# Attention and a routed expert layer on one core: the first five shared steps inside attention's last five, a third group routed in attention

## The chip, the cores and the metric

One core of a Trainium2 chip runs the whole kernel as one program. The metric is the device time of a run in microseconds (us). Five engines work side by side, each through a queue of its own in order: PE (products and transposes), ACT (activations and copies), DVE (vector operations), POOL (some vector work, and the indirect DMAs) and SP (plain DMAs). They meet only at semaphores.

## What is computed

```python
def reference(x, ctx, Wq, Wk, Wv, Wo, bo, gate_w, gate_b, w1, b1, w3, b3, w2, b2, sw1, ...):
    # x (4, 1024, 256), ctx (4, 64, 192), 16 heads of 64, 8 experts, top 2, H = 352, all fp32
    x = x + xattn(layernorm(x), ctx)          # cross attention, softmax over 64 keys
    xf = layernorm(x).reshape(4096, 256)
    scores = softmax(xf @ gate_w.T)           # (4096, 8)
    idx = top_k(scores + gate_b, 2)
    rw = zeros((4096, 8)).at[arange, idx].add(scores[idx])
    h = silu((xf @ w1[e] + b1[e]) * (xf @ w3[e] + b3[e]))
    y = sum_e rw[:, e] * (h @ w2[e] + b2[e])
    z = silu((xf @ sw1 + sb1) * (xf @ sw3 + sb3)) @ sw2 + sb2     # shared expert, all tokens
    return x + y + z
```

## The kernel before

The 4096 tokens are 32 tiles of 128 (NT = 32). Every product is done as three products of rounded parts: each operand is split into a high part (`...h`, an ACT copy to fp32r) and a low part (`...l`, DVE: the value less the high part).

After a short prelude, which folds the weights into `AU`, comes **attention**, a software pipeline written out in steps s = 0 to 37 (`tile_step`, lag 6). Every engine goes through the same steps. In step s PE does the scores of tile s-1, the gate product of tile s-6 (L1309, out of `xn2T`), the transposes of the probabilities of tile s-3, the output product of tile s-4 and, last, the transposes of the normalised tile s-5 (L1360, `xn2`). ACT copies `xn2T` (L740), makes `xn2` (L747), `pTh` (L768) and the exponentials. DVE does maxima and sums, `pTl`, the residual and the statistics, and copies the logits (L1007). POOL computes the reciprocal roots (L601 to L605) and normalises the probabilities (`prob`, L612, once a step). SP loads `xin`, `xres`, and stores. From step 33 on no scores are left: the last five steps, 33 to 37, are the drain.

**Routing** of a group of tiles is six stages on DVE (`route`), one a step, each a chain in which every operation waits for the one before (`link`). Its stage 1 needs an exponential of ACT, stage 5 the running counts of PE (`ranks`). At its end the slots are cast, and POOL scatters two records a tile into the table `slots_scratch` (L658, at most three in flight). Groups 0 to 7 and 8 to 15 run in steps 14 to 19 and 22 to 27. The other 16 tiles, the rest, are routed after attention. Scatters go at one tile a step from step 20, and stop in step 30 with tile 10.

Idle places in attention also take the expert weights: SP loads `w13_raw` (steps 13 to 17, 21 to 23) and `w2_raw` (24 to 32), ACT makes `w13h` of experts 0 to 4 in steps 33 to 37 (L871), DVE `w13l` of experts 0 to 2 in 35 to 37 (L1120).

**The FFN** is 103 steps of one tile (`unit_step`): 20 shared tiles, 71 routed units of 128 gathered rows, 12 shared tiles. In step s PE does the second product of tile s-4 (nine matmuls), the transposes of tile s (L1407, into bank 0), the transposes of the hidden rows of s-3 (L1415), the first product of tile s-1 (twelve matmuls). ACT copies `yrow` of s-4, `uxTh` of s, `hTh` of s-3, and does Silu of s-2; DVE `uxTl`, `hTl`, `uv` (L1161) and `hid` (L1164). In steps 1 to 17 ACT and DVE also split the other weights (`high2`, `low2`, `high13`, `low13`).

PE starts the FFN when all of attention is done, and puts the rest's `ranks` behind its step 2; DVE puts the rest's stages between its steps 0 to 3. After the last scatter SP reads each unit's slots (L534), POOL gathers the rows (L707), and PE's step 20, the first of a routed unit, waits for the first gather. The scatters that are left over after attention stand in this loop of POOL, those of tiles 11 to 15 first:

```python
            for t in range(scattered_by(NT), REST[0]):
                for k in range(TOP):
                    scatter_record(t, k)
            pool.wait_ge(slot_ok, len(GROUPS) + 1)
```

## Time and profile before

| | |
|---|---|
| median of 3 runs | 738.7 us (736.76 to 742.82) |
| the profiled execution | 745.34 us, its span 743.6 us |
| granted TensorE clock, mean | 0.977 |
| PE busy | 676.8 us (91%) |
| DVE busy | 527.4 us (71%) |
| POOL busy | 431.5 us (58%) |
| ACT busy | 402.4 us (54%) |
| attention's last gate product | 335.19 us from the span's start |
| first routed step on PE | 427.18 us |

The busy share counts what an engine executes, waits left out; PE's is modelled and says that it had a matmul in its pipe, not that it ran at its peak. The chain of waits goes back from the last instruction to what released each one. Times in the rows are from the span's start.

### The profile page before, as it was taken

What the parts mean: (1) busy time and instruction counts of PE and PEld (TensorE: products, weight loads), DVE (VectorE), ACT (ScalarE), POOL (GpSimd) and SP (SyncE); (2) the same over time, 40 slices, a digit from 0 to 9 for tenths busy, and PEclk for the clock granted to TensorE, in tenths of its full rate; (3) what the DMA queues carried; (4) which work ended last, traced back from release to release, by engine and by line L of the source; (5) the groups of instructions that cost most, each with busy time, mean ns of one, the idle gap of its engine ahead of it and who ended that gap; (6) DMA issues with size and microseconds to landing.
All of it is one profiled execution on the core that took longest, in us unless ns stands there. A gap on an engine that the chain in (4) does not pass through costs nothing.

```text
span 743.6 us, 16844 instructions
## 1 busy us (share of the span) xinstructions
PE 676.8 (91%) x4645; PEld 632.3 (85%) x4646; DVE 527.4 (71%) x1080; ACT 402.4 (54%) x1307; POOL 431.5 (58%) x514
## 2 busy tenths in 40 slices
PE   4996799999898989966799599999999999999996
PEld 3785699998897879865799599999999999999995
DVE  4875788888976868747789456666666666666686
ACT  3985778777766657655543234444444444444342
POOL 5352674545567768434546417776676777676273
PEclk9999999999999999987999889999999999999999
DMA  8202222235427756426241125554444444455496
GB/s 243 81 1 71 65 76 83 83 109 176 120 58 140 128 111 108 124 76 188 46 70 37 36 61 73 75 76 73 74 76 71 71 71 73 75 96 104 91 386 253
DMA packets 71940, 74.83 MB, mean 101 GB/s; under 512 B 21178, under 2 KB 65572, under 8 KB 71876
## 3 DMA queue, kind: packets, MB, share of 16 engines
q1 hardware_dynamic: 52372, 50.51, 26.0%
q0 software_dynamic: 15760, 18.96, 15.9%
q10 hardware_dynamic: 3744, 4.59, 1.8%
q8 instruction: 30, 0.49, 0.3%
q14 instruction: 34, 0.28, 0.1%
HBM read 47.22 MB, written 26.81 MB: 100 GB/s over the span
## 4 chain that ended last, share of the span: by engine, by line
PE 75%; DMA 11%; issue 4%; DVE 4%; POOL 3%; ACT 2%; SPq 0%; ACTq 0%; POOLq 0%; DVEq 0%
PE ps L1235 62%; DMA slots_scratch<-record,slot 8%; PE ps L1415 4%; PE ps L1332 3%; PE ps L1407 3%; POOL slots_scratch L658 2%; DMA xin<-in_x 1%; PE ps L1309 1%; DMA wq_sb<-in_L_xattn_Wq 1%; PE ps L1322 1%; ACT prob L776 1%; DVE hmax L1021 1%; PE ps L1360 1%; DVE st L1056 0%; DVE x L1054 0%
## 5 line engine op out<-in xcount | busy, mean ns | idle before, releaser
L714 POOL DMA_INDIRECT acc_scratch<-yrow,slots x71 | 112.1, 1579 | 71.0 <-ACT yrow L902 70.7
L902 ACT ACTIVATE yrow<-ps,slots 128x256 f32<-128x256 f32 x71 | 33.8, 476 | 147.8 <-PE ps L1235 133.2
L1235 PE MATMUL ps<-AU,xTh 128*128 128x512 f32 x256 | 96.8, 423 | 9.2 <-DVE xTl L1034 9.2
L1235 PE MATMUL ps<-AU,pTh 128*128 128x256 f32 x512 | 101.3, 290 | 0.0
L1235 PE MATMUL ps<-w13h,uxTh 128*128 x284 | 97.7, 344 | 0.0
L1161 DVE TENSOR_TENSOR uv<-ps,b 128x704 f32<-128x704 f32 x71 | 63.3, 892 | 47.6 <-PE ps L1235 45.8
L658 POOL DMA_INDIRECT slots_scratch<-record,slot x64 | 67.5, 1054 | 45.0 <-DMA slots_scratch<-record,slot 32.6
L1235 PE MATMUL ps<-w13h,uxTl 128*128 x284 | 91.6, 322 | 0.0
L1235 PE MATMUL ps<-w13l,uxTh 128*128 x284 | 91.3, 321 | 0.0
L707 POOL DMA_INDIRECT xrow<-xn_scratch,slots x71 | 69.9, 985 | 26.3 <-issue 20.7
L1235 PEld LDWEIGHTS ps<-AU,pTh 128*128 128x128 f32 x512 | 82.4, 191 | 0.0
L776 ACT ACTIVATE prob<-ps,nmax 128x64 f32<-128x64 f32 x256 | 76.7, 338 | 6.8 <-DVE nmax L1024 6.8
L1143 DVE TENSOR_TENSOR uxTl<-ps,uxTh 128x256 fp32r<-128x256 f32 x103 | 43.6, 423 | 51.1 <-ACT uxTh L916 42.4
L1235 PE MATMUL ps<-AU,pTl 128*128 128x256 f32 x256 | 72.8, 284 | 0.0
L612 POOL TENSOR_TENSOR prob<-prob,hinv 128x1024 f32<-128x1024 f32 x32 | 61.0, 1905 | 19.4 <-DVE hinv L1003 19.3
L1235 PEld LDWEIGHTS ps<-AU,xTh 128*128 128x128 f32 x256 | 49.6, 194 | 19.1 <-DVE xTl L1034 10.2
L1235 PE MATMUL ps<-w2h,hTh 128*128 x213 | 63.0, 296 | 0.0
L1164 DVE TENSOR_TENSOR hid<-uv 128x352 f32<-128x352 f32 x103 | 59.9, 581 | 3.5
L1235 PE MATMUL ps<-w2l,hTh 128*128 x213 | 60.3, 283 | 0.0
L1235 PE MATMUL ps<-w2h,hTl 128*128 x213 | 60.0, 282 | 0.0
L776 ACT ACTIVATION_READ_ACCUMULATOR prob<-ps,nmax 128x1 f32 x256 | 59.2, 231 | 0.0
L1148 DVE TENSOR_TENSOR hTl<-ps,hTh 128x384 fp32r<-128x384 f32 x103 | 57.2, 556 | 1.8 <-ACT hTh L921 1.4
(237 smaller groups left out, 1989.3 us busy)
## 6 DMA issues: line engine op xcount, KB each, us to landing
sums<-acc_scratch SPq DMA_DIRECT2D x16, 512.0 KB, 10.5
w_raw<-in_L_ffn_w SPq DMA_DIRECT2D x16, 352.0 KB, 4.1
xin<-in_x SPq DMA_DIRECT2D x32, 128.0 KB
xres<-in_x SPq DMA_DIRECT2D x32, 128.0 KB
acc_scratch<-x SPq DMA_DIRECT2D x32, 128.0 KB
xn_scratch<-xn SPq DMA_DIRECT2D x32, 128.0 KB
xrow<-xn_scratch SPq DMA_DIRECT2D x32, 128.0 KB, 3.1
out_x<-sums SPq DMA_DIRECT2D x7, 512.0 KB, 12.0
```

Source lines behind the costliest of these rows:

```text
L612: pool.tensor_tensor(heads, heads, hinv[:, p, :].unsqueeze(2).to_broadcast([P, HEADS, NK]), ALU.mult).then_inc(norm_ok, 1)
L658: pool.indirect_dma_start(slots_dram, bass.IndirectOffsetOnAxis(ap=slot[:, k, t:t + 1], axis=0), record[:, t, k, :], None).then_inc(scat_o ...
L707: pool.indirect_dma_start(xrow[:, m, :], None, xn2_dram, bass.IndirectOffsetOnAxis(ap=slots[:, u, 0:1], axis=0)).then_inc(gather_in[m], 16)
L714: pool.indirect_dma_start(acc_dram[u % 2], bass.IndirectOffsetOnAxis(ap=slots[:, u, 0:1], axis=0), yrow[:, m % YRING, :], None, compute_op ...
L776: act.activation(prob[:, p, h * NK:(h + 1) * NK], ps[:, s_bank(p) + h // 8, h % 8 * NK:(h % 8 + 1) * NK], ACT.Exp, bias=nmax[:, p, h - HS: ...
L902: act.activation(yrow[:, y, :], ps[:, 6 + m % 2, 0:D], ACT.Copy, scale=slots[:, bass.ds(u, 1), 1].bitcast(F32)).then_inc(y_ok, 1)
L1143: dve.tensor_tensor(uxTl[:, p, :], ps[:, 0, 0:D], f32(uxTh[:, p, :]), ALU.subtract).then_inc(uxTl_ok, 1)
L1148: dve.tensor_tensor(hTl[:, :], ps[:, 5, 0:H3], f32(hTh[:, :]), ALU.subtract).then_inc(hTl_ok, 1)
L1161: dve.tensor_tensor(uv[:, :, :], ps[:, 1 + 2 * p:3 + 2 * p, 0:H], bias, ALU.add).then_inc(bias_ok, 1)
L1164: dve.tensor_tensor(hid[:, p, 0:H], uv[:, 0, :], uv[:, 1, :], ALU.mult).then_inc(z_ok, 1)
L1235: last = pe.matmul(out, stationary(k, a), moving(k, b), start=(k == 0 and i == 0), stop=(k == n - 1 and i == len(PARTS) - 1 and not more))
L1415: last = pe.transpose(ps[:, 5, k * P:(k + 1) * P], hid[:, p, k * P:(k + 1) * P], ident[:, :])
```

## The change

- **Shared steps in the drain.** `DRAIN` = 33. In attention's steps 33 to 37 every engine does, after its part of attention, the FFN's step s-33. PE's transposes of the first five shared tiles go to bank 7 instead of bank 0 (`x_bank`). PE then does steps 5 to 7 before the rest's `ranks`; DVE puts the rest's stages between its steps 5 to 8. `hid`'s padding is set by POOL in step 33.
- **A third group.** Tiles 16 to 19 are routed in steps 28 to 33 (`BEGIN`); the rest is 12 tiles.
- **Scatters** go on through step 36: tiles 0 to 16 in attention, 17 to 19 right after it, 20 to 31 when the rest's slots are there.
- **Loads and splits.** w1 and w3 of experts 5 to 7 are loaded one half a step in steps 20 to 25 (before: whole in 21 to 23), w2 in 26 to 33. `high2` moves from FFN steps 1 to 4 to 5 to 8, `low13` of experts 3 and 4 to steps 6 and 7, `low2` to 8 to 15. Shared rows 8 to 11 are loaded ahead of the biases.
- **Layout.** `xres`, `x2`, `xn2`, `xn2T` move below `xin`, `b13` and `gv` move up.

```diff
-    GROUPS = ((0, 8), (8, 16))
-    REST = (16, NT)
-    NREST = NT - 16
+    GROUPS = ((0, 8), (8, 16), (16, 20))
+    BEGIN = (14, 22, 28)
+    REST = (20, NT)
+    NREST = NT - 20
...
+        DRAIN = NT + 1
+        XBANK7 = NT + 6 - DRAIN
...
+        def x_bank(t):
+
+            return 7 if isinstance(t, int) and t < XBANK7 else 0
...
-                if s in (21, 22, 23):
-                    load_w13(s - 16)
...
+                if 20 <= s < 20 + 2 * (E - EARLY13):
+                    load_w13((s - 20) // 2 + EARLY13, s % 2)
...
-                for s in range(min(step, NT - 2) + 1):
-                    routed = max([b for _, b in GROUPS if b + 6 + STAGES <= s], default=0)
+                for s in range(step + 1):
+                    routed = max([b for (_, b), first in zip(GROUPS, BEGIN) if first + STAGES <= s], default=0)
...
-            for t in range(scattered_by(NT), REST[0]):
+            for t in range(scattered_by(NT + 4), REST[0]):
+                pool.wait_ge(slot_ok, len(GROUPS))
...
                 tile_step(s, par)
+                if s >= DRAIN:
+                    unit_step(s - DRAIN, s - DRAIN)
                 if 33 <= s < 33 + EARLY13:
                     high13(s - 33)
...
             act.wait_ge(lg_ok, NT)
-            act.wait_ge(hid_one, 2)
-            act.wait_ge(zero_out, 16 * (NB // QUAD + 3))
-            unit_steps(act, unit_step)
+            for half in xn2_out + x2_out:
+                act.wait_ge(half, before(NT))
+            act.wait_ge(rt_sub, len(GROUPS) + 1)
+            act.activation(rest_score[:, :, :], rest_marked[:, 0, :, :], ACT.Exp).then_inc(rt_exp, 1)
+            unit_steps(act, unit_step, begun=NT + 6 - DRAIN)
...
+            def begin_step(s, par):
+                tile_step(s, par)
+                if s == DRAIN:
+                    pe.wait_ge(exp_ok, NT)
+                    pe.wait_ge(sw_lo, 2)
+                if s >= DRAIN:
+                    unit_step(s - DRAIN, s - DRAIN)
+
+            steps(NT, 0, 6, begin_step)
             pe.wait_ge(lg_ok, NT)
-            pe.wait_ge(sw_lo, 2)
-            for s in range(3):
+            for s in range(NT + 6 - DRAIN, 8):
                 unit_step(s, s)
             pe.wait_ge(chosen_ok, len(GROUPS) + 1)
+            pe.wait_ge(shared_row_ok, 4)
             ranks(7, rest_chosen, NREST).then_inc(rank_ok, 1)
```

Where the instructions stand is best seen in the queues. First ACT in attention's steps 35 and 36 (the row of `xn2T` begins a step; `xn<-x` is `xn2`; `w13h` is the pair of copies of one expert). Before:

```order
L740 ACTIVATE xn2T<-ps 128x256 [waits R_ok,T2_ok]
L747 ACTIVATE xn<-x,nm,rs 128x256 [waits xn2_out_even,T2_ok,nm2_ok]
L871 ACTIVATE w13h<-w_raw 128x704 [waits O_ok,raw13_in2]
L871 ACTIVATE w13h<-w_raw 128x704
L740 ACTIVATE xn2T<-ps 128x256 [waits R_ok,T2_ok]
```

Changed, step 35 and the first two of step 36 (`uxTh` and `hid` belong to shared step 2):

```order
L753 ACTIVATE xn2T<-ps 128x256 [waits R_ok,T2_ok]
L760 ACTIVATE xn<-x,nm,rs 128x256 [waits xn2_out_even,T2_ok,nm2_ok]
L927 ACTIVATE uxTh<-ps 128x256 [waits UV_ok,X_ok]
L937 ACT_TABLE_LOAD
L937 ACTIVATE hid<-hid 128x352 [waits z_ok]
L886 ACTIVATE w13h<-w_raw 128x704 [waits O_ok,raw13_in2]
L886 ACTIVATE w13h<-w_raw 128x704
L753 ACTIVATE xn2T<-ps 128x256 [waits R_ok,T2_ok]
```

The pair of copies has moved behind `uxTh` and the first Silu with its table load, and all of these stand ahead of the next `xn2T`.

Then ACT at the end of attention, from the last expert's pair to the first Silu behind the rest's exponential (`rest_score`). Before:

```order
L871 ACTIVATE w13h<-w_raw 128x704 [waits O_ok,raw13_in4]
L871 ACTIVATE w13h<-w_raw 128x704
L882 ACTIVATE rest_score<-rest_marked 128x128 [waits rt_sub]
L916 ACTIVATE uxTh<-ps 128x256 [waits zero_out,X_ok,hid_one,lg_ok]
L916 ACTIVATE uxTh<-ps 128x256 [waits X_ok]
L876 ACTIVATE w2h<-w_raw 128x768 [waits raw2_in0] x2
L916 ACTIVATE uxTh<-ps 128x256 [waits UV_ok,X_ok]
L926 ACT_TABLE_LOAD
L926 ACTIVATE hid<-hid 128x352 [waits z_ok]
```

Changed:

```order
L886 ACTIVATE w13h<-w_raw 128x704 [waits O_ok,raw13_in4]
L886 ACTIVATE w13h<-w_raw 128x704
L950 ACT_TABLE_LOAD [waits x2_out_even,x2_out_odd,xn2_out_odd,rt_sub,xn2_out_even]
L950 ACTIVATE rest_score<-rest_marked 128x96 [waits lg_ok]
L895 DMA acc_scratch<-yrow 128x256 [waits shared_row_ok]
L918 ACTIVATE yrow<-ps 128x256 [waits Y_ok]
L927 ACTIVATE uxTh<-ps 128x256 [waits UV_ok,X_ok]
L932 ACTIVATE hTh<-ps 128x384 [waits Y_ok,H_ok]
L937 ACT_TABLE_LOAD
L937 ACTIVATE hid<-hid 128x352 [waits z_ok]
L891 ACTIVATE w2h<-w_raw 128x768 [waits raw2_in0] x2
```

The exponential has moved behind Silu steps, so a table load stands before it and another behind, ahead of the next Silu.

Last DVE from the last logits to the rest's second stage. Before:

```order
L1007 COPY logits<-ps 128x8 [waits R_ok]
L1120 TENSOR_TENSOR w13l<-w_raw,w13h 128x704 [waits w13_hi] x2
L1180 MEMSET rest_chosen 128x4 [waits O_ok,lg_ok]
L970 TENSOR_REDUCE rest_v<-logits 128x16 [waits rt]
L971 TENSOR_TENSOR rest_marked<-logits,rest_v 128x128 [waits rt]
L1143 TENSOR_TENSOR uxTl<-ps,uxTh 128x256 [waits uxTh_ok,hid_one]
L974 TENSOR_REDUCE rest_v<-rest_score 128x16 [waits rt_exp]
```

Changed, with shared step 4 (`uxTl`, `hTl`, `uv`, `hid`) and the pair of expert 2 ahead of the rest's first operation:

```order
L1022 COPY logits<-ps 128x8 [waits R_ok]
L1159 TENSOR_TENSOR uxTl<-ps,uxTh 128x256 [waits UV_ok,uxTh_ok]
L1164 TENSOR_TENSOR hTl<-ps,hTh 128x384 [waits Y_ok,hTh_ok]
L1177 TENSOR_TENSOR uv<-ps,bs 128x704 [waits z_ok,UV_ok]
L1180 TENSOR_TENSOR hid<-uv 128x352 [waits H_ok,bias_ok]
L1139 TENSOR_TENSOR w13l<-w_raw,w13h 128x704 [waits w13_hi] x2
L1200 MEMSET rest_chosen 128x4 [waits O_ok,lg_ok]
L985 TENSOR_REDUCE rest_v<-logits 128x12 [waits rt]
L986 TENSOR_TENSOR rest_marked<-logits,rest_v 128x96 [waits rt]
L1159 TENSOR_TENSOR uxTl<-ps,uxTh 128x256 [waits UV_ok,uxTh_ok]
L1164 TENSOR_TENSOR hTl<-ps,hTh 128x384 [waits Y_ok,hTh_ok]
L1177 TENSOR_TENSOR uv<-ps,bs 128x704 [waits z_ok,UV_ok]
L1180 TENSOR_TENSOR hid<-uv 128x352 [waits H_ok,bias_ok]
L989 TENSOR_REDUCE rest_v<-rest_score 128x12 [waits rt_exp]
```

Between the last logits and the rest a whole shared step has come in, and another, step 5, between the subtraction and the first operation that needs the exponential.

## Rows read from the trace of the kernel before

**Rows 1.** The chain of waits that ended last: start, us, what (merged pieces).

```profile
424.02 2.95 DMA xrow<-xn_scratch,slots
...
434.19 3.00 PE ps L1235 x21
```

**Rows 2.** PE timeline: start us, us, line, operation, count, idle time before it and releaser.

```profile
319.74 0.61 PE L1309 MATMUL ps<-gateT,xn2T 128*128 128x8 f32 x4 [0.47 <-ACT xn2T L740]
...
329.12 0.61 PE L1309 MATMUL ps<-gateT,xn2T 128*128 128x8 f32 x4 [0.47 <-ACT xn2T L740]
...
333.57 0.69 PE L1360 MATMUL ps<-ident,xn 128*128 128x128 f32 x2 [3.83 <-ACT xn L747]
...
335.19 1.02 PE L1309 MATMUL ps<-gateT,xn2T 128*128 128x8 f32 x4 [0.94 <-ACT xn2T L740]
...
347.92 0.70 PE L1286 MATMUL ps<-rest_chosen,ones 128*128 128x128 bf16 x16
...
373.49 0.39 PE L1235 MATMUL ps<-ws2h,hTh 128*128 128x256 f32 x1 [1.87 <-DVE hTl L1148]
...
427.18 0.69 PE L1407 MATMUL ps<-ident,xrow 128*128 128x128 f32 x2 [7.77 <-DMA xrow<-xn_scratch,slots]
```

**Rows 3.** POOL timeline from the end of attention to the first gather.

```profile
337.29 1.66 POOL L658 DMA_INDIRECT slots_scratch<-record,slot  x1 [0.41 <-issue]
...
358.09 0.96 POOL L658 DMA_INDIRECT slots_scratch<-record,slot  x1 [1.91 <-DMA slots_scratch<-record,slot]
...
361.55 0.96 POOL L658 DMA_INDIRECT slots_scratch<-record,slot  x1 [0.30 <-issue]
...
372.18 1.29 POOL L658 DMA_INDIRECT slots_scratch<-record,slot  x1 [2.66 <-DMA slots_scratch<-record,slot]
...
418.36 0.96 POOL L658 DMA_INDIRECT slots_scratch<-record,slot  x1 [0.30 <-issue]
```

**Rows 4.** DVE timeline from the last logits to the rest's slots.

```profile
336.25 0.17 DVE L1007 COPY logits<-ps 128x8 f32<-128x8 f32 x1 [3.43 <-PE ps L1309]
...
336.34 1.68 DVE L1120 TENSOR_TENSOR w13l<-w_raw,w13h 128x704 fp32r<-128x704 f32 x2
...
337.97 0.06 DVE L1180 MEMSET rest_chosen<- 128x4 uint32 x1
...
351.75 0.18 DVE L993 CAST slot<-rest_v 128x32 int32<-128x32 f32 x1
...
354.00 0.16 DVE L1202 TENSOR_TENSOR sums<-carry,region 128x8 f32<-128x8 f32 x1
```

**Rows 5.** ACT timeline around attention's last steps.

```profile
317.44 1.47 ACT L871 ACTIVATE w13h<-w_raw 128x704 fp32r<-128x704 f32 x2
...
319.30 0.39 ACT L740 ACTIVATE xn2T<-ps 128x256 f32<-128x256 f32 x1 [0.38 <-PE ps L1360]
...
344.98 1.28 ACT L926 ACT_TABLE_LOAD   x1
...
346.28 0.50 ACT L926 ACTIVATE hid<-hid 128x352 f32<-128x352 f32 x1
```

**Rows 6.** Windows of PE: stretch, us, busy (instructions), granted clock, DMA share, GB/s.

```profile
268.00:271.70 3.70, 0.91 (x9) 1.00 1.04 77
271.70:276.00 4.30, 4.21 (x30) 0.62 0.37 107
```

**Rows 7.** POOL timeline, one normalisation a step; and the chain's piece on `xin`.

```profile
160.78 1.91 POOL L612 TENSOR_TENSOR prob<-prob,hinv 128x1024 f32<-128x1024 f32 x1
...
209.72 1.90 POOL L612 TENSOR_TENSOR prob<-prob,hinv 128x1024 f32<-128x1024 f32 x1 [0.72 <-DVE hinv L1003]
...
224.13 1.91 POOL L612 TENSOR_TENSOR prob<-prob,hinv 128x1024 f32<-128x1024 f32 x1
...
279.90 1.91 POOL L612 TENSOR_TENSOR prob<-prob,hinv 128x1024 f32<-128x1024 f32 x1 [0.71 <-DVE hinv L1003]
...
225.33 10.77 DMA xin<-in_x
```

More of the change, by code:

```diff
@@ L145, in xattn_moe @@
         Uh, Ul = (AU[:, :, i, :].rearrange("p b (j d) -> p b j d", j=NJ) for i in (2, 3))
+        pre = ExitStack()
+        raw = ExitStack()
+        wv_raw = sb("wv_raw", [P, 2, INNER], F32, raw)
+        raw.close()
+        wvl = sb("wvl", [P, 2, INNER], F32R, pre)
+        pre.close()
+        xres = sb("xres", [P, 2, D], F32, att)
+        x2 = sb("x2", [P, 2, D], F32, att)
+        xn2 = sb("xn2", [P, 2, D], F32, att)
+        xn2T = sb("xn2T", [P, 2, D], F32, att)
         xin = sb("xin", [P, 2, D], F32, att)
@@ L526, in _ @@
             sp.wait_ge(x2_ok, NT)
+            for t in range(RING, RING + 4):
+                shared_x(t)
             for e in range(E):
@@ L534, in unit_slots @@
                 sp.dma_start(slots[:, u, :], slots_dram[bass.ds(row, P), :]).then_inc(slots_in[u % RING], 16)
-            for t in range(RING, NA):
+            for t in range(RING + 4, NA):
                 shared_x(t)
@@ L715, in scatter_add @@
                                         yrow[:, m % YRING, :], None, compute_op=ALU.add).then_inc(y_out[u % 2], 16)
+            for half in xn2_out + x2_out:
+                pool.wait_ge(half, before(NT))
             ahead = RING - 2
@@ L876, in high2 @@
                 act.activation(flat[0], flat[1], ACT.Copy).then_inc(w2_hi, 1)
-            act.wait_ge(zero_ok, 1)
-            steps(NT, 1, 6, begin_step, begun=0)
-            act.wait_ge(rt_sub, len(GROUPS) + 1)
-            act.activation(rest_score[:, :, :], rest_marked[:, 0, :, :], ACT.Exp).then_inc(rt_exp, 1)
             def shared_z(t):
@@ L915, in unit_step @@
                     wait(act, UV_ok, t - 1)
-                    act.activation(uxTh[:, p, :], ps[:, 0, 0:D], ACT.Copy).then_inc(uxTh_ok, 1)
+                    act.activation(uxTh[:, p, :], ps[:, x_bank(t), 0:D], ACT.Copy).then_inc(uxTh_ok, 1)
                 t = s - 3
@@ L1104, in begin_step @@
                 for g, (a, b) in enumerate(GROUPS):
[L1105 removed]
+                    stage = s - BEGIN[g]
                     if stage == 0 and g == 0:
```

108 lines of the change are left out of this document (56 added, 52 removed).

## The prediction

> **What bounds the kernel now.** I read the chain that ended last first. Behind 428 us it is nothing but PE, one step of 3.0 us of products after another with 0.5 us of transposes between them; ahead of that it hangs on the DMAs `slots_scratch<-record`, then on reading the slots and on the gather [rows 1]. So the kernel has one gate: the routed steps can't begin before all 64 record scatters have landed. PE came to routed step 0 (step 20 of the FFN) 7.8 us too early and began it at 427.18 [rows 2]. Behind that lie 83 steps at PE's own pace, which the change leaves alone, so **the time moves by what the gate moves**.
>
> Then POOL's timeline, which issues the scatters [rows 3]. The first 22 ran inside attention. The other 42 began only after attention: 337.29 to 418.36, 41 gaps of 1.98 us; one issue with the pause ahead of it is 0.96 + 0.30 = 1.26, the rest is waiting for the DMA three before. From the last start to PE's start it is 8.8 us. The last 24 began at 372.18, 23 gaps of 2.01 us. Ten of the 42 (tiles 11 to 15) covered the routing of the rest: its slots were cast by 351.93 [rows 4], the eleventh scatter, the first to need them, went at 358.09. In the old kernel late routing costs nothing up to about 357.
>
> **What the change makes of the gate.** 34 scatters go inside attention's steps instead of 22, and 6 (tiles 17 to 19) right after it. That leaves the 24 of tiles 20 to 31, and these need the rest's slots with nothing in front to cover them. In the old trace the same 24 began at 372.18. So the question is one number: **R, when DVE casts the rest's slots. The gate moves by R + 0.3 - 372.2.** It was 351.9; there are 20 us to lose, and I find nearly all lost.
>
> *The drain, up to the last logits.* I go by ACT's order. In old steps 33 to 37 a pair of `w13h` copies (1.47 us) ran while PE was in its products, so `xn2T` followed the transpose by 0.05 and PE's gate product followed that: in steps 34, 36 and 37 at 319.74, 329.12 and 335.19 [rows 2, 5]; in step 35 it was about 324.8. Now `uxTh` of the shared step stands before the pair, and it waits for a transpose that PE does last in its step. The pair therefore lands between PE's transpose and `xn2T`. By step, in old times:
> - 33: ranks of the third group on PE (sixteen such products take 0.70 at the rest, [rows 2], four 0.2, and DVE's copy is waited for): about 1.0, an estimate. Transpose ends 319.9, X of shared step 0 at 320.6, `uxTh` 321.0, the pair 322.4, `xn2T` 322.8: gate product at 322.85, +3.1.
> - 34: PE has 2.2 more (X 0.25, and 1.9 for the twelve longer ones of the 21 products that take 3.00, [rows 1]), ACT 2.5: gate product 330.4, +5.6.
> - 35: the first Silu with its table load, 1.28 + 0.50, stands ahead of the pair too: 338.7, +9.6.
> - 36: the 3.83 that PE idled for `xn2` of tile 31 is now filled; against that X, three transposes and products (2.4), `uxTh`, `hTh`, Silu, pair: 343.7, +8.6.
> - DVE has a `w13l` pair (1.66) ahead of that last logits copy: 346.0 instead of 336.25, +9.8 [rows 4].
>
> *To the first instruction of the rest.* DVE stood at it after one pair, 337.97. Now shared step 4 stands there: its `uv` waits for PE's products (3.5 us after the logits), `hid`, a pair: 350.9, +12.9.
>
> *The rest's routing.* It took 13.9 (337.97 to 351.93), 33 instructions on DVE: 7.9 of 26 routing operations, 4.1 of seven that belong to shared steps 0 to 2, which were not yet full, and 1.9 of waits. Now: routing 6.9 (each 0.04 shorter with 12 tiles instead of 16, an estimate); full steps 5, 6, 7 at 2.1 (351.93 to 354.00), 6.4; two `w13l` pairs 3.3; waits 3.5, since ACT must load the Exp table (1.28) after DVE's subtraction, does Exp, and only then `uxTh`, and PE, which stood 3 us meanwhile, has a halved clock afterwards. That it would is read from 268 to 276: 2.8 us of idleness, then 0.62 of the clock over 4.3 us, so that most of that stretch ran at 1.2 GHz instead of 2.4 [rows 6]. Sum 20.1, so R = 371.0.
>
> *The Trainium skill on that table load.* The row shows 1.28 for the load, and Silu starts 0.02 behind its end [rows 5]. "ScalarE: Activation LUTs", What ACT_TABLE_LOAD costs, adds a drain of about 1.38 us to every switch. With three switches in the new order instead of one, two or three of them in this chain, R would be some 3 to 4 later by that rule; by the row it is 371.0. I go by the row.
>
> *The third group inside attention.* The normalisation (one per step) ticks at 7.2 to 7.4 us. Over the six steps of group one it took 48.9 from 160.78 to 209.72, 4.5 more than six times 7.4; over group two 55.8 from 224.13, 12.6 more than six times 7.2 [rows 7]. Of the latter 3.6 is an `xin` that took 10.77 us to land beside the w1/w3 loads, 3.6 longer than a step. Group three has four tiles instead of eight and its rank stage falls in the drain, where I have booked it. I take +2.5, a little over half of group one; the bounds are 0 (the stages fit beside PE's work, as in single steps of group one) and +12. The w1/w3 loads of the last three experts now come one half per step over six steps: I take back about half of the 3.6, -2 (bounds 0 and -4).
>
> *Sum.* R = 371.0 + 2.5 - 2.0 = 371.5, first of the 24 at 371.8 against 372.18: -0.4. The queue is empty by then, so the first three go at 1.26 instead of 2.01: -1.5. **The gate moves by -1.9.** Does PE come later than that? It began step 8 at 373.49 and step 20 at 427.18 - 7.77 = 419.4, 3.83 per step [rows 2]; now it has step 8 at about 367 and would stand at step 20 at 413 to 417, 8 to 12 us before the gate at 425.3. It is no limit. The loads and layout moves elsewhere (shared rows 8 to 11 before the biases, `hid` set in step 33, the moved tiles) are costed at nothing: POOL has 30 us of slack there and the rows are needed four steps later; were they late they would delay only PE, which waits anyway. The profiled execution took 745.3 with a span of 743.6, 0.9% above the median 738.7, so I set the difference against the median: 738.7 - 1.9 = 736.8, **737.0** in round numbers.
>
> **Rivals.**
> - *The shared steps fit into the drain's gaps (faster).* If ACT's pair does not block, only PE's added work counts: 1.0 + 2.2 + 2.2 + 2.4 = 7.8, against idle times of some 7 in steps 33 to 37, 3.83 of it in one piece [rows 2]. The last logits would come 1 to 2 later instead of 9.8, R about 363, the gate -10: 729. If DVE also kept 13.9 for the rest, R is 356, and the gate is 357 + 46.2 - 1.5 + 8.8 = 410.5; PE would come to step 20 at about 405 to 409: -14 to -17, 723. For it speaks that engines idle there much; against it the order in their queues. Chance 0.28, most of it above 727.
> - *The third group collides as the second did (slower).* The place is steps 28 to 33, the mechanism DVE's link of dependent operations before `hsum`, beside w2 loads, with late ranks and then a halved clock, as at 268 to 276 [rows 6]. Price: +8 to +12 instead of +0.5 net. Since R has no slack left, all of it counts once R passes 372.2: 745 to 749. For it: w2 loads and scatters lie in these steps too. Against it: it has half the tiles, and `xin` is no longer awaited from step 30 on. Chance 0.17.
> - *The table rule of the Trainium skill holds.* As a mechanism: after each switch the next activation starts 1.4 us later than in the row; twice or three times in the chain, 740.5. The row speaks against it: 0.04.
> - *My forecast*, R within 367 to 377: 732 to 742. Chance 0.51.
>
> **Numbers.** About 1% is what a measurement of this kernel can tell from no change: 731.3 and 746.1. Faster by over 1%: nearly all of the first rival and a little of mine, 0.29. Slower: most of the second rival's, 0.13. Same: 0.58. The range takes the first rival's single step (726) and the second's lower price (748).
>
> **What the new profile would show.** The 24 last scatters begin near 372, the 6 before them end over 15 us earlier and POOL stands in between; the last logits copy is near 346, the slots near 372; `w13h` pairs lie right behind `uxTh` and PE idles 1 to 2 us before the gate products of steps 34 to 36; PE waits 8 us or more for the first gather, which starts near 425. I am wrong if the scatters run on without a hole, if the last logits come before 340, if the pace of the 24 is far from 2.0, or if the norm ticks of steps 28 to 33 exceed 7.2 by more than a microsecond each.

## The result and the profile after

The changed kernel took **745.68 us** (median of 17 runs, 741.16 to 756.88 and one of 2687), the kernel before in the same comparison 741.28 (17 runs). Ratio **1.0061, 95% interval 1.0033 to 1.0089**: 0.3 to 0.9% slower. Forecast were 737.0 us and 0.2% faster, with the time in the range 726 to 748. The changed kernel was compared three more times, unedited, with the kernel before: 0.9945 [0.9904, 0.9986], 1.0021 [0.9977, 1.0064] and 0.9999 [0.9962, 1.0036]. The four don't agree within their intervals; their plain mean is 1.0007. So the change moves the time by less than two comparisons of one and the same pair differ. The medians in these four are 745.7, 741.5, 742.6 and 741.5 for the changed kernel and 741.3, 745.2, 740.6 and 742.4 for the one before: the 1.0061 comes with a late median of the changed kernel, the 0.9945 with a late one of the kernel before. Disturbed executions, four of the changed kernel's 17 among them, are left out of all ratios, and the second repeat of the changed kernel and the repeat of the one before, whose profiled executions were such, are not in the table below.

The profiled execution of the changed kernel took 741.25 us, its span is 739.5. These rows of PE's timeline answer to [rows 2] (start us, us, line, operation, count, idle time before it and releaser). The first five are the gate products of steps 33 to 37:

```profile
318.39 0.61 PE L1328 MATMUL ps<-gateT,xn2T 128*128 128x8 f32 x4 [1.95 <-ACT xn2T L753]
...
327.03 0.61 PE L1328 MATMUL ps<-gateT,xn2T 128*128 128x8 f32 x4 [2.10 <-ACT xn2T L753]
...
333.98 0.61 PE L1328 MATMUL ps<-gateT,xn2T 128*128 128x8 f32 x4 [0.20 <-ACT xn2T L753]
...
341.92 0.61 PE L1328 MATMUL ps<-gateT,xn2T 128*128 128x8 f32 x4 [1.99 <-ACT xn2T L753]
...
347.49 0.51 PE L1328 MATMUL ps<-gateT,xn2T 128*128 128x8 f32 x4
...
358.58 0.39 PE L1254 MATMUL ps<-ws2h,hTh 128*128 128x256 f32 x1 [3.09 <-DVE hTl L1164]
...
371.04 0.63 PE L1426 MATMUL ps<-ident,xrow 128*128 128x128 f32 x2
376.11 0.38 PE L1426 MATMUL ps<-ident,xrow 128*128 128x128 f32 x2
383.67 0.63 PE L1426 MATMUL ps<-ident,xrow 128*128 128x128 f32 x2
388.95 0.38 PE L1426 MATMUL ps<-ident,xrow 128*128 128x128 f32 x2
392.49 0.38 PE L1426 MATMUL ps<-ident,xrow 128*128 128x128 f32 x2
...
424.29 0.44 PE L1426 MATMUL ps<-ident,xrow 128*128 128x128 f32 x2 [1.10 <-DMA xrow<-xn_scratch,slots]
```

The last row is the gate: 424.29 instead of 427.18, with **1.10 us of idle time ahead of it instead of 7.77**. The transposes from 371.04 to 388.95 belong to shared steps 8 to 11; they are 5 to 7.6 us apart, those behind them 3.5 to 4.3. POOL's timeline (as [rows 3]) shows the hole in the scatters:

```profile
351.07 0.96 POOL L672 DMA_INDIRECT slots_scratch<-record,slot  x1 [0.30 <-issue]
374.33 0.96 POOL L672 DMA_INDIRECT slots_scratch<-record,slot  x1 [22.29 <-DVE slot L1008]
...
414.54 0.96 POOL L672 DMA_INDIRECT slots_scratch<-record,slot  x1 [0.30 <-issue]
421.17 0.99 POOL L718 DMA_INDIRECT xrow<-xn_scratch,slots  x1 [5.67 <-DMA slots<-slots_scratch]
```

DVE's timeline from the last logits to the rest's slots and on to shared step 9 (as [rows 4]), and ACT's around the Exp (as [rows 5]):

```profile
350.66 0.16 DVE L1022 COPY logits<-ps 128x8 f32<-128x8 f32 x1
...
353.05 1.69 DVE L1139 TENSOR_TENSOR w13l<-w_raw,w13h 128x704 fp32r<-128x704 f32 x2
354.68 0.06 DVE L1200 MEMSET rest_chosen<- 128x4 uint32 x1
...
373.87 0.18 DVE L1008 CAST slot<-rest_v 128x24 int32<-128x24 f32 x1
...
376.60 0.95 DVE L1145 TENSOR_TENSOR w2l<-w_raw,w2h 128x768 fp32r<-128x768 f32 x1
377.46 0.16 DVE L1221 TENSOR_TENSOR sums<-carry,region 128x8 f32<-128x8 f32 x1
...
379.87 0.74 DVE L1229 TENSOR_REDUCE units<-passed 128x71 f32<-128x568 f32 x1
380.64 0.42 DVE L1159 TENSOR_TENSOR uxTl<-ps,uxTh 128x256 fp32r<-128x256 f32 x1
```

```profile
355.44 1.28 ACT L950 ACT_TABLE_LOAD   x1 [3.44 <-DVE rest_marked L986]
...
357.95 1.28 ACT L937 ACT_TABLE_LOAD   x1
359.25 0.50 ACT L937 ACTIVATE hid<-hid 128x352 f32<-128x352 f32 x1
```

Between shared steps 8 and 9 DVE does a `w2l` split (0.95) and then the first part of the maths of the units, which works out each unit's expert and rows (377.46 to 380.64, 3.2 us), before it turns to step 9's `uxTl`. Between steps 9 and 10 there is another such pair, 0.95 and 3.2.

The chain that ended last has changed too. In the kernel before it ran through the scatters' DMAs, 8.3% of the span. In this execution it doesn't: it goes through DVE and PE in the last shared steps, where each waits for the other (start us, us, what).

```profile
414.12 1.34 PE ps L1254 x9
...
421.34 0.46 DVE hTl L1164
```

In the two repeats with a profile in the table the chain runs through the scatters again (4.9 and 4.5%).

POOL's normalisations of steps 20, 28 and 33 (as [rows 7]):

```profile
215.47 1.90 POOL L626 TENSOR_TENSOR prob<-prob,hinv 128x1024 f32<-128x1024 f32 x1 [0.72 <-DVE hinv L1018]
...
280.58 1.90 POOL L626 TENSOR_TENSOR prob<-prob,hinv 128x1024 f32<-128x1024 f32 x1 [0.72 <-DVE hinv L1018]
...
319.39 1.90 POOL L626 TENSOR_TENSOR prob<-prob,hinv 128x1024 f32<-128x1024 f32 x1 [0.27 <-DVE hinv L1018]
```

### The profile page after: what moved, and what is told of

It is laid out like the page before. It is cut to its first block, busy times and chain, and to the rows that moved or that the text cites. A ratio compares the mean times of both kernels' runs of the same rounds, so it can differ in the third digit from the quotient of the medians.

```text
span 739.5 us, 16893 instructions
## 1 busy us (share of the span) xinstructions
PE 682.0 (92%) x4646; PEld 636.3 (86%) x4647; DVE 532.2 (72%) x1107; ACT 405.4 (55%) x1310; POOL 428.1 (58%) x514
## 4 chain that ended last, share of the span: by engine, by line
PE 81%; DVE 8%; issue 4%; ACT 2%; DMA 2%; another core or an unknown queue 1%; SPq 0%; POOL 0%; DVEq 0%; ACTq 0%; POOLq 0%
PE ps L1254 67%; PE ps L1436 4%; PE ps L1351 3%; PE ps L1426 3%; PE ps L1328 1%; DMA xin<-in_x 1%; DVE uv L1177 1%; DMA wq_sb<-in_L_xattn_Wq 1%; PE ps L1341 1%; DVE hTl L1164 1%; DVE hmax L1036 1%; DVE w13l L1139 1%; PE ps L1379 1%; ACT prob L789 1%; ACT w13h L886 1%
## 5 line engine op out<-in xcount | busy, mean ns | idle before, releaser
L725 POOL DMA_INDIRECT acc_scratch<-yrow,slots x71 | 112.1, 1579 | 70.5 <-ACT yrow L911 70.2
L1254 PE MATMUL ps<-AU,xTh 128*128 128x512 f32 x256 | 98.5, 430 | 8.6 <-DVE xTl L1049 8.6
L718 POOL DMA_INDIRECT xrow<-xn_scratch,slots x71 | 69.8, 983 | 27.0 <-issue 20.4
## 6 DMA issues: line engine op xcount, KB each, us to landing
sums<-acc_scratch SPq DMA_DIRECT2D x16, 512.0 KB, 10.5
```

The source lines that it names most:

```text
L718: pool.indirect_dma_start(xrow[:, m, :], None, xn2_dram, bass.IndirectOffsetOnAxis(ap=slots[:, u, 0:1], axis=0)).then_inc(gather_in[m], 16)
L725: pool.indirect_dma_start(acc_dram[u % 2], bass.IndirectOffsetOnAxis(ap=slots[:, u, 0:1], axis=0), yrow[:, m % YRING, :], None, compute_op ...
L1254: last = pe.matmul(out, stationary(k, a), moving(k, b), start=(k == 0 and i == 0), stop=(k == n - 1 and i == len(PARTS) - 1 and not more))
```

## The experiments

The table has one row for each profile, read from the same places: the time from the normalisation of step 20 to that of step 28; when the cast of the rest's slots ends; when the last scatter starts; when PE stands ready for step 20 (start of its first routed transpose less its idle time); when that transpose starts (the gate); the time of the profiled execution; the median of all runs; the ratio to the kernel before. All times in us.

| kernel | 20 to 28 | slots | last scatter | PE ready | gate | profiled | median | ratio [95%] |
|---|---|---|---|---|---|---|---|---|
| before | 70.2 | 351.9 | 418.4 | 419.4 | 427.2 | 745.3 | 741.3 | 1 |
| changed | 65.1 | 374.1 | 414.5 | 423.2 | 424.3 | 741.3 | 745.7 | 1.0061 [1.0033, 1.0089] |
| changed, repeated | 62.8 | 371.3 | 413.7 | 419.5 | 422.9 | 740.1 | 741.5 | 0.9945 [0.9904, 0.9986] |
| changed, third repeat | 64.3 | 372.7 | 415.5 | 422.2 | 426.0 | 742.4 | 741.5 | 0.9999 [0.9962, 1.0036] |
| places only | 67.0 | 353.8 | 417.3 | 418.3 | 425.9 | 744.0 | 744.2 | 1.0011 [0.9975, 1.0046] |
| loads only | 63.1 | 349.6 | 414.3 | 414.0 | 423.7 | 740.1 | 739.9 | 1.0002 [0.9967, 1.0037] |
| third group only | 66.0 | 353.4 | 400.8 | 418.9 | 418.9 | 733.9 | 737.9 | 0.9994 [0.9957, 1.0032] |
| no third group | 64.6 | 372.3 | 423.3 | 425.1 | 432.8 | 750.1 | 750.0 | 1.0123 [1.0053, 1.0192] |
| pair first | 65.1 | 365.7 | 407.7 | 413.5 | 417.0 | 733.1 | 736.5 | 0.9880 [0.9847, 0.9912] |
| splits later | 64.5 | 366.6 | 409.1 | 423.1 | 423.1 | 738.0 | 737.5 | 0.9948 [0.9911, 0.9985] |
| splits spread | 63.7 | 358.5 | 400.7 | 407.2 | 410.4 | 727.3 | 734.6 | 0.9913 [0.9881, 0.9944] |
| Exp early | 63.1 | 364.3 | 406.1 | 413.1 | 415.6 | 731.5 | 733.4 | 0.9899 [0.9847, 0.9952] |

Two columns carry most of what follows. From the gate to the end of the span it is 314.1 to 316.4 us in every row in which PE waits at the gate (before: 743.6 - 427.2 = 316.4), and a run takes 1.7 to 1.8 more than its span. So **a time is its gate plus 317.2**, give or take 1.3. And one profiled execution can lie 7 us from its kernel's median (splits spread: 727.3 and 734.6), so a difference of two single profiles is no measurement of a few microseconds.

**1. The two kernels repeated.**

> The changed kernel once more, nothing altered. In its first profile PE ran with half the clock from 43 to 54 us, in the middle of the prelude and with no idle time before it, which cost 4.4 us (96 products in 18.1 instead of 13.7 us); the gate (first routed transpose on PE) was at 424.3 against 427.2. Theory A (the dip belongs to this kernel): it is there again, and the time is 1.006 of the kernel before. Theory B (the dip comes and goes in either kernel): it may be absent, and then the span is near 735, with a gate near 419; the median is above the kernel before for another reason, which lies between 320 and 425 us and must show there.

> The kernel before once more, nothing altered. Theory A: no dip of the clock between 20 and 60 us, ratio 1.000 with a spread of its runs under 1%. Theory B: a dip there in some of the profiles; ratio 1.000 too, gate near 427.

The changed kernel gave 0.9945, the kernel before, against itself, 0.9982 [0.9944, 1.0021]. The stretch at half the clock was there in both profiles, 13.7 us long in the changed kernel and 10.2 in the one before, so theory B holds as far as the dip goes: it does not belong to one kernel, and it came once with 1.0061 and once with 0.9945. A second and a third repeat of the changed kernel:

> The changed kernel a third time, since two measurements disagree: 1.006 and 0.9945 of the kernel before. If the difference is drawn from the clock's dips, which come at other places in each execution, this one lies between; the stretches behind the prelude should repeat: 65 us or less from tick 20 to tick 28, 31 from tick 33 to the last logits, 23.4 from there to the slots, 24 scatters at 1.8.

> The changed kernel once more, unedited, on the same chip as the three above. If its gate is PE-bound without slack, its ratio lies within 0.994 to 1.006 as in the three measurements so far (1.0061, 0.9945, 1.0021), with the stretch from step 33 to the slots 54 to 55 us, 36 us for the shared steps 8 to 16, and the routed transpose 1 to 4 us behind PE's arrival. If the spread of its ratio comes from the chip and not from the kernel, the half-clock stretch in the prelude (41 to 57 us) and the clock from 320 to 425 us tell it apart.

They gave 1.0021 and 0.9999. In the first and the third repeat the gate is at 422.9 and 426.0 with 3.4 and 3.8 us of idle time ahead of it. The stretch from step 33 to the slots is 54.7, 54.5 and 55.6 us in the three profiles of the table: the order of the drain gives the same length each time. The 0.6% of the first comparison did not come again, and I can't say what made it. The chip alone is not the reason for the spread: 0.9945 and 0.9999 were measured on the same one.

**2. The places of the buffers only** (the kernel before with the new buffer layout, and ACT waiting for attention's stores ahead of the rest's Exp).

```diff
+        xres = sb("xres", [P, 2, D], F32, att)
+        x2 = sb("x2", [P, 2, D], F32, att)
...
+        gv = sb("gv", [P, 6, 8], F32)
...
+            for half in xn2_out + x2_out:
+                act.wait_ge(half, before(NT))
             act.wait_ge(rt_sub, len(GROUPS) + 1)
```

> The kernel before with only the new places of the buffers (and ACT waiting for the stores of x2 and xn2 ahead of the rest's exponential, which should be done by then). Theory A, in the form that the moved buffers bring the dip: half the clock around 45 us and 1.005 or more. Theory B: 1.000, and attention's steps as in the kernel before.

1.0011 [0.9975, 1.0046]: the places cost nothing that can be measured, though half the clock was there for 6.8 us from 41 us on. It has the old order throughout, and still shows 67.0 us from step 20 to 28 where the kernel before showed 70.2, and a gate 1.3 earlier. That is the scatter between executions of one order.

**3. The loads only** (the kernel before with the new schedule of w1, w3 and w2).

```diff
-                if s in (21, 22, 23):
-                    load_w13(s - 16)
-                if 24 <= s < 24 + EARLY2:
-                    load_w2(s - 24)
+                if 20 <= s < 20 + 2 * (E - EARLY13):
+                    load_w13((s - 20) // 2 + EARLY13, s % 2)
+                if 26 <= s < 26 + EARLY2:
+                    load_w2(s - 26)
```

> The kernel before with only the new schedule of the expert weights' loads (first loads one w1/w3 half each in the steps from 20 on, w2 from step 26). Theory (loads): two earlier traces of the kernel before took 66.0 to 71.1 us from the norm tick of step 20 to that of step 28, the changed kernel's 62.8 to 65.1 with the same code of the steps but other loads; if the loads are the cause, this kernel shows 63 to 66 us there, its last slots and its first gather come 4 to 5 us earlier relative to step 2's tick than the 352 to 353 of the kernel before, and the ratio is 0.993 to 0.996. Rival (the gain in those steps belongs to something else that the change does): 70 us there, ratio 1.000. Second rival: the loads now end later and the first experts' weights are late, visible as PE waiting for w13 in the routed steps: stretch from the first routed transpose to the end above 317 us and ratio above 1.002.

The mark was hit: 63.1 us, and all nine profiles of the table with the new loads show 62.8 to 65.1, the three with the old ones 66.0 to 70.2. The time was missed: 1.0002 [0.9967, 1.0037]. Against the 67.0 and 66.0 of the other two with old loads the gain is about 3 us, 0.4%, just what the interval can hide; the 7 us against the first profile of before are not there. From the gate to the end of the span it is 314.6 us, so the second rival, late weights, is out.

**4. The third group without shared steps in the drain, and the reverse.** First the kernel before with the new places, the third group and the scatters going on:

```diff
+    GROUPS = ((0, 8), (8, 16), (16, 20))
+    BEGIN = (14, 22, 28)
+    REST = (20, NT)
...
-                for s in range(min(step, NT - 2) + 1):
+                for s in range(step + 1):
```

> The kernel before with the new places of the buffers, the third group in steps 28 to 33 and the scatters going on to step 36, but no shared step in the drain and the old loads. Theory (the gate is the later of two chains: scatters, and PE's twenty shared steps): the slots of the rest come about 16 us after the last logits as before, the scatters then run without a hole and the last one starts near 400, but PE does its 20 shared steps after attention and reaches step 20 no sooner than 103.5 us behind tick 33 (before: 427.18 - 7.77 - 315.9). Gate about 104 us behind tick 33, PE waits under 2 us for the gather; with 2 us more for the group, 0.992 to 0.996 of the kernel before. Rival (the scatters alone set the gate): it comes 10 us or more earlier, ratio 0.985.

Then the changed kernel with the third group taken back:

```diff
-    GROUPS = ((0, 8), (8, 16), (16, 20))
-    BEGIN = (14, 22, 28)
-    REST = (20, NT)
+    GROUPS = ((0, 8), (8, 16))
+    BEGIN = (14, 22)
+    REST = (16, NT)
```

> The changed kernel without the third group: the rest is 16 tiles again, all else as changed. Theory: the shared steps in the drain delay the slots of the rest (55 us behind tick 33 instead of 36), and 32 scatters at 1.8 us now stand behind them instead of 24, so the first routed step comes about 121 us behind tick 33 (changed 105, before 111) and PE waits over 12 us for the gather; steps 28 to 33 take 36.0 us instead of 37.3 to 38.8. Ratio 1.004 to 1.010 of the kernel before. Rival (the drain's shared steps bring the gain by themselves): ratio under 0.995.

With the third group alone the last scatter starts at 400.8, 17.6 earlier than before, and the time is 0.9994 [0.9957, 1.0032]. The scatters no longer set the gate; PE does. In its profile the first routed transpose stands at 418.88 with no wait for a gather, 0.5 us ahead of where PE stood ready in the kernel before. The marks were as expected (102.0 us behind step 33's normalisation), the ratio of 0.992 to 0.996 was missed. Without the third group but with the shared steps in the drain it is 1.0123 [1.0053, 1.0192]: the slots come at 372.3, and now 32 scatters instead of 24 lie behind them. PE waits 7.67 us again:

```profile
372.12 0.18 DVE L1008 CAST slot<-rest_v 128x32 int32<-128x32 f32 x1
```

```profile
372.60 1.05 POOL L672 DMA_INDIRECT slots_scratch<-record,slot  x1 [35.95 <-DVE slot L1008]
...
423.29 0.96 POOL L672 DMA_INDIRECT slots_scratch<-record,slot  x1 [0.30 <-issue]
```

```profile
432.81 0.69 PE L1426 MATMUL ps<-ident,xrow 128*128 128x128 f32 x2 [7.67 <-DMA xrow<-xn_scratch,slots]
```

(DVE, POOL and PE of that kernel.) Here I had expected more than 12 us of waiting: the scatters went faster than the 1.8 us assumed, 1.64 each over 32, and the ratio lies above the 1.004 to 1.010 that I had expected, with four runs behind it. Each half of the change brings nothing or costs by itself: one frees the scatters and leaves PE, the other holds the slots up.

The shared steps in the drain did not bring PE forward either. Counted from step 33's normalisation PE stands ready for step 20 at 103.8, 102.7 and 105.1 us in the changed kernel and at 108.5 without the third group; in the old order it was 103.5 (before), 100.5 (places only and loads only) and 102.0 (third group only). The five steps that PE no longer has behind attention are lost again in a drain that is 10.7 us longer and in slower steps behind it.

**5. ACT's weight pair ahead of the shared step** (changed kernel, two blocks exchanged).

```diff
-                if s >= DRAIN:
-                    unit_step(s - DRAIN, s - DRAIN)
                 if 33 <= s < 33 + EARLY13:
                     high13(s - 33)
+                if s >= DRAIN:
+                    unit_step(s - DRAIN, s - DRAIN)
```

> The changed kernel with ACT's pair of w13h copies ahead of the shared step instead of behind it in steps 33 to 37. Theory of the prediction (the pair behind uxTh holds up the gate product): the waits of the gate product for xn2T (2.10, 0.20, 1.99 us) fall to under 0.6, the last logits come 3 to 5 us earlier, the slots of the rest too, and since PE is at most 1 us from being the limit at the gate, the time falls by 2 to 4 us against the changed kernel. Rival (PE's own added work sets the drain): the last logits move by less than 1.5 us and the time by nothing.

0.9880 [0.9847, 0.9912], beside the changed kernel's 0.9945 on the same chip at the same time. ACT's timeline shows the pair lying in what was idle time before `uxTh`, and `xn2T` starting 0.28 after `uxTh` where the changed kernel had 1.46 us of pair between them; PE's waits for `xn2T` in steps 34 to 36 fall from 2.10, 0.20 and 1.99 to 0.75, none and 0.64 (I had expected less than 0.6):

```profile
321.34 1.47 ACT L886 ACTIVATE w13h<-w_raw 128x704 fp32r<-128x704 f32 x2
323.43 0.39 ACT L927 ACTIVATE uxTh<-ps 128x256 fp32r<-128x256 f32 x1 [0.62 <-PE ps L1426]
323.71 0.38 ACT L753 ACTIVATE xn2T<-ps 128x256 f32<-128x256 f32 x1
```

```profile
318.54 0.61 PE L1328 MATMUL ps<-gateT,xn2T 128*128 128x8 f32 x4 [0.75 <-ACT xn2T L753]
```

From the normalisation of step 33 to the last logits it is 27.4 us, in the changed kernel 31.3 (31.1 and 31.0 in the repeats), in the kernel before 20.4. So the forecast's mechanism of the drain is real: the pair is worth 4 of the 10.7 by which the drain grew. The other 7 stay when the pair is out of the way; they come with the shared steps and, 0.7 of them as the third-group kernel's 21.1 shows, with the group's `ranks`.

**6. VectorE's splits out of the way** (VectorE is DVE, ScalarE is ACT). Three kernels on top of the fifth. In the first, the splits of experts 2 to 4 leave step 37 and shared steps 6 and 7 and join those of experts 5 to 7, so that steps 16 to 18 have two each:

```diff
-                if s >= 35:
+                if 35 <= s < 37:
                     low13(s - 35)
...
-                if isinstance(s, int) and 6 <= s < 8:
-                    low13(s - 3)
...
+                if isinstance(s, int) and 8 + E <= s < 8 + E + 3:
+                    low13(2 * (s - 8 - E) + 2)
+                    low13(2 * (s - 8 - E) + 3)
```

> The pair-first kernel, in which DVE also puts off three w13l pairs: those of experts 2, 3 and 4 leave step 37 and the shared steps 6 and 7 and come in twos in steps 16 to 18. Theory (DVE's queue sets the slots): they come 3 x 1.66 = 5 us earlier, 19 us or less behind the last logits instead of 24.4. PE becomes the limit of the gate then (it was 3.5 us ahead of it), so 1 to 4 us are gained against the pair-first kernel: 0.983 to 0.988 of the kernel before. Rival: the work put off comes back one for one in steps 16 to 18, PE waits there for hTl, and the time is that of the pair-first kernel.

0.9948 [0.9911, 0.9985]. The slots come 20.2 us behind the last logits instead of 24.4 (19 or less was expected), but the two pairs in one step hold PE there. PE stands ready only at 423.1, and waits 18.5 us for `hTl` between 340 and 424. Its last shared steps are 5.4 us apart:

```profile
412.41 0.38 PE L1425 MATMUL ps<-ident,xrow 128*128 128x128 f32 x2
417.77 0.38 PE L1425 MATMUL ps<-ident,xrow 128*128 128x128 f32 x2
423.14 0.38 PE L1425 MATMUL ps<-ident,xrow 128*128 128x128 f32 x2
```

In its own comparison the changed kernel had 1.0021, so against that it is at 0.993, just where the pair-first kernel is too (0.9880 against 0.9945): the rival is what happened.

In the second the w1/w3 splits of experts 2 to 7 go one to a step, and the w2 splits two to a step between them:

```diff
-                if isinstance(s, int) and 8 <= s < 8 + E:
-                    low2(s - 8)
...
+                if isinstance(s, int) and s in (10, 12, 14, 16, 18, 19):
+                    low13(2 + (10, 12, 14, 16, 18, 19).index(s))
+                if isinstance(s, int) and s in (11, 13, 15, 17):
+                    low2(s - 11)
+                    low2(s - 10)
```

> The changed kernel with ScalarE's weight pairs behind the shared activation (as in the fourth experiment, 0.988) and with VectorE's weight splits spread out: the w1/w3 remainders of experts 2 to 7 in steps 10, 12, 14, 16, 18, 19 of the shared steps and two w2 remainders each in steps 11, 13, 15, 17; none in attention's last step or in shared steps 6 to 9. Theory (VectorE's queue is what makes PE late at step 20): PE's eight shared steps from 8 to 16 take 31 to 33 us instead of the 36 of the changed kernel, the slots are read 3 to 5 us earlier after the last logits than the 24.4 of the experiment it builds on, and the gate, counted from step 2's tick, is at 335 to 338 us instead of 339.2; ratio 0.983 to 0.990. Rival (the splits are work that must be done anyhow and the later place only moves PE's wait): the 8 to 16 stretch is 31 to 33 but 16 to 20 is longer by as much, gate 339 to 341, ratio 0.988 to 0.993.

(The kernel at 0.988 is the fifth experiment here, and in it the pairs stand ahead of the shared step.) It gave 0.9913 [0.9881, 0.9944], in a comparison where the changed kernel had 0.9999; the ratio lies in the rival's range. In its profile the slots come 18.6 us behind the last logits (5.8 less than in the fifth), PE is ready at 407.2, and the wait for `hTl` is 6.1 us in all:

```profile
L1253 PE MATMUL ps<-ws2h,hTh 128*128 128x256 f32 x57 | 17.6, 309 | 6.3 <-DVE hTl L1164 6.1
```

(PE's groups from 340 to 424: busy us, mean ns, idle before and releaser.) The changed kernel has 10.1 in the same view. Shared steps 8 to 16 took 34.3 us, 35.2 in the pair-first kernel and 36.5, 35.6 and 36.0 in the changed one, not the 31 to 33 I had expected. The maths of the units still stands on DVE in steps 8 and 9, and the transposes of steps 9, 10 and 11 are still 5.9 and 5.2 us apart. The rival's reason, that the wait only moves on, is not what the profile shows: step 16 to PE ready took 15.9 against the pair-first kernel's 15.7. PE still waits 3.2 us for the gather, so the scatters behind the slots still set the gate.

In the third, the first stage of the rest's routing and its Exp stand ahead of shared step 4:

```diff
+                if s == NT + 5:
...
+                    act.wait_ge(rt_sub, len(GROUPS) + 1)
+                    act.activation(rest_score[:, :, :], rest_marked[:, 0, :, :], ACT.Exp).then_inc(rt_exp, 1)
...
+                if s == NT + 5:
...
+                    link(dve.memset(rest_chosen[:, NREST, :], 0.0))
+                    rest(0)
```

> As the kernel above, and the first stage of the last tiles' routing (VectorE) and its exponential (ScalarE) stand ahead of the fifth shared step's work instead of behind it. Theory: the clearing of the rest's choices starts within 0.2 us of the last logits instead of 4.0 to 4.4 us behind them, so slots, scatters and gather are 3 to 4 us earlier than in the kernel above; but the gate is then PE's own arrival at step 20, since its transposes do not wait for the gather: the first routed transpose gains less than 1.5 us and the ratio is within 0.003 of that kernel. Rival (the scatters still set the gate): the gate gains the whole 3 to 4 us, ratio lower by 0.004 to 0.005.

0.9899 [0.9847, 0.9952]: not to be told from the second kernel, as the theory said. Its reason was wrong. The clearing did start right behind the last logits (341.41 after 341.18), but the slots came 22.9 us behind it instead of 16.1. ACT's timeline has both table loads ahead of the shared step's activation now, with ACT idle before them:

```profile
342.15 1.28 ACT L871 ACT_TABLE_LOAD   x1 [4.63 <-DVE rest_marked L987]
343.44 0.28 ACT L871 ACTIVATE rest_score<-rest_marked 128x96 f32<-128x96 f32 x1
343.89 0.38 ACT L933 ACTIVATE uxTh<-ps 128x256 fp32r<-128x256 f32 x1
344.67 1.28 ACT L943 ACT_TABLE_LOAD   x1
345.96 0.50 ACT L943 ACTIVATE hid<-hid 128x352 f32<-128x352 f32 x1
```

PE's transposes of shared steps 4 and 5 are 7.9 us apart there, 3.9 without it. What was won at the front was lost in the step behind it.

## Why the prediction was right or wrong

The sign was wrong by the first comparison, and by all four together the change is worth nothing that can be measured. The range held 745.68. The step that failed is the last one, the base from which the 1.9 us were taken; the cover that PE was given was mis-sized too. Step by step:

- **One gate, and the time moves by what it moves: right.** What lies behind the gate is constant within 2.3 us over all kernels in which PE waits there.
- **R, the rest's slots: 371.5 forecast, 374.1, 371.3 and 372.7 measured.** The last logits: 346.0 forecast, 350.7, 347.9 and 348.1. Much of these offsets comes from ahead of the change. From the normalisation of step 33 to the slots the forecast has 371.0 - 315.9 = 55.1; measured were 54.5 to 55.6. The gate products of steps 34 to 37 were forecast 7.0, 14.5, 22.8 and 27.8 us behind that normalisation and stood at 7.6, 14.6, 22.5 and 28.1. The order of the queues, read by hand, gave them within a microsecond. The waits for `xn2T` in steps 34 to 36, forecast as 1 to 2 us, were 2.10, 0.20 and 1.99; the 1.95 of step 33 is not the drain's, the kernel with the third group alone has 1.93 there.
- **The halved clock in the rest's routing: a premise that two of three profiles don't bear out.** PE stood 3.09 us before 358.58 and was granted the full clock from there to 370 us; in the first repeat it was the same, to 368. In the third repeat it was at 0.50 from 358 to 360, and there the slots came 1.2 us later behind the last logits. DVE waited 2.3 us in that routing, where 3.5 were booked.
- **Third group +2.5: right.** Steps 28 to 33 took 36.0 us in the old kernels without it and 36.2 in the changed kernel without it, 37.2 to 38.8 in those with it: 1.2 to 2.8 more. The rival in which it collides for +8 to +12 is out.
- **Loads -2: too small by the profiles, not to be decided by the times.** 3 to 5 us in the stretch, 0 within 2.6 us in the time.
- **The queue's pace of 2.01: too slow.** The 24 scatters took 40.2 us from first to last start (414.5 - 374.3), 1.75 each; 46.2 was their time before, 44.7 my figure for them. In the profiles of the table with the shared steps in the drain the pace of the last 24 was 1.72 to 1.85, in the old ones 1.79 to 2.02: a pace read from one execution had 10% of play, 5 us over 24. On the other side, from the last scatter to the gate it was 9.2 to 10.5 us in the changed kernel where I had 8.8. That the gate came within 1.0, 2.4 and 0.7 us of the forecast 425.3 is in part luck: later slots in two of them and a longer tail in all made up for the faster queue.
- **The table load: by the row.** Silu follows its load at 359.25, 0.02 behind the load's end (357.95 + 1.28). The 1.38 of drain for every switch that the Trainium skill states ("ScalarE: Activation LUTs", What ACT_TABLE_LOAD costs) is not seen here either.
- **"It is no limit", PE at step 20: mis-sized.** I had PE at step 8 at about 367 and at step 20 at 413 to 417, with 8 to 12 us of cover. It began step 8 at 369.8 (367.1 and 369.2 in the repeats) and was ready for step 20 at 423.2 (419.5 and 422.2): 52.5 to 53.4 us instead of 46. The pace was taken from the wrong steps. I gave PE the 3.83 us that the old steps from 8 on had. But the slow steps, with the routing of the rest and the maths of the units on DVE between them, are moved by five with everything else: in the old kernel they were 0 to 7, in the new one 5 to 10. The three steps from 8 to 11 took 17.9 us, where the old pace gives 11.5 and the old steps themselves 10.6; DVE has 3.2 us of the maths of the units and a `w2l` split in each of two of them. With 17.9 for these and 3.83 for the other nine, PE is ready at 367 + 17.9 + 34.5 = 419.4, and the 8 to 12 us of cover are 6 or less. So two chains end at nearly the same time, the scatters and PE: PE's lead is 1.1, 3.4 and 3.8 us instead of 7.8, and in the execution with 1.1 the chain that ended last runs through DVE and PE. In all three the first routed transpose still waited for the gather, so this step did not make the forecast of the gate wrong.
- **The difference set against the median: the step that failed.** The sum was made from a profiled execution of 745.3 and its gate of 427.2, and the 1.9 us were then taken from 738.7. But by "gate plus 317.2", an estimate from the table, a run of the 17 runs' median of 741.3 has its gate at about 424.1. So the profiled run's gate was some 3 us late, and in the stretch from step 20 to 28 it was 3 to 4 us longer than the two other profiles with old loads; and the 738.7 of three runs lay 2.6 under what 17 runs gave. My gate for the new kernel was 425.3. Read as a time by itself that is 425.3 + 317.2 = 742.5, 0.2% slower than 741.3, and the three repeats' medians are 741.5, 742.6 and 741.5. I had forecast where the gate would come within 2.4 us, and turned it into a time 5.5 us too low by subtracting from a baseline in which the excess was not contained. Of the 8.7 us between 737.0 and 745.68 that leaves 3.2 with no cause shown.

The rival *the shared steps fit into the gaps* is out as it stands (the slots are at 371 to 374, not 356 to 363). In the fifth and sixth experiments ACT's and DVE's weight work no longer stands ahead of the drain's short chain, and the slots are at 358.5. That is not the rival come true by its own reason: 46.1 us behind step 33's normalisation, against 54.5 to 55.6 and 36.0 before, it is R = 362 in the old kernel's times, but the last logits still come 7.2 us later than before and not 1 to 2.

Open: why the same pair of kernels compares at 1.0061 once and 0.9945 another time. The kernels' runs scatter alike (standard deviations 2.8 to 3.6 us for the changed one, 2.7 to 3.4 for the one before), so it isn't shown that the lost lead of PE makes the changed kernel more easily disturbed; that was a guess of mine which these runs don't support.

Four versions beat both kernels: the changed kernel with the pair first (0.9880, median 736.5), with the splits later (0.9948, 737.5), with the splits spread (0.9913, 734.6), and with the Exp early as well (0.9899, 733.4). Against the changed kernel in the same comparison they are 0.65% (0.9880 against 0.9945), 0.7% (0.9948 against 1.0021), 0.9% and 1.0% faster (0.9913 and 0.9899 against 0.9999), and with 0.3 to 0.5% of play in each ratio they can't be told from each other. The exchange of two blocks in the first of them has most of the gain.

## What to carry to other kernels

When a change makes the binding chain shorter, cost the second chain to the same gate with the same care: renumber the slow steps with the move, rather than give the moved steps the pace of those that held their numbers before. Work with no deadline of its own (splits of weights for later) belongs in an engine's idle time ahead of a wait, one piece to a step; behind a wait it stands in everybody's chain, and two in one step become a chain of their own. And a sum made on one profiled execution gives a time for the new kernel (its gate plus the constant rest); taking the difference to the median of a few runs adds the profile's own lateness to the gain.

## What the runs showed of the hardware

The granted clock of TensorE falls to its half in the prelude while PE is fully busy, and in the 3 us before it PE was busy without a break. These are windows of PE (stretch, us, busy with instructions, granted clock, DMA share, GB/s) of the changed kernel, then of the kernel before, in the same code:

```profile
40.00:43.00 3.00, 3.00 (x17) 1.00 0.00 0
43.00:46.00 3.00, 3.00 (x13) 0.53 0.00 0
46.00:50.00 4.00, 4.00 (x18) 0.50 0.00 0
50.00:54.00 4.00, 4.00 (x20) 0.57 0.00 0
54.00:57.00 3.00, 3.00 (x25) 1.00 0.03 5
```

```profile
46.00:50.00 4.00, 4.00 (x30) 1.00 0.00 0
50.00:54.00 4.00, 4.00 (x33) 1.00 0.01 4
```

The three rows with 0.50 to 0.57 are mostly time at 1.2 GHz instead of 2.4, and PE was busy throughout, before and in them. In the chain of waits the 96 products that lie there take 18.11 us in the changed kernel, 13.70 in the one before and 18.11 in that one's repeat (start us, us, what):

```profile
43.16 18.11 PE ps L1254 x96
```

```profile
43.45 13.70 PE ps L1235 x96
```

```profile
43.53 18.11 PE ps L1235 x96
```

The length of this stretch differs from profile to profile of the same code: none and 10.2 us in the kernel before and its repeat, 10.2, 13.7 and 10.2 in the changed kernel's three in the table, none without the third group, 3.4 to 6.8 in the others, of which four have the changed kernel's prelude. So 4.4 us between two executions can come without any change, and they stand ahead of everything that the forecast speaks of. What makes it fall there no run shows.
